# Attention 2: where the next group's weights are split, and on which engine their low parts are made

## The chip, the cores and the metric

The kernel runs on one core of a Trainium2 chip. Its metric is the device time of one execution, in microseconds. The kernel before takes 973.61 us, the median of three runs (972.61 to 974.28).

A core has five instruction streams that run at the same time and meet only at semaphores: TensorE (PE in the profile, its weight loads are PEld), VectorE (DVE), ScalarE (ACT), GpSimd (POOL) and SyncE (SP), which here only issues DMAs. Each stream runs its instructions in the order in which they were written. An instruction that waits holds up all that stands behind it on its engine.

## The reference, cut to what matters

The program is a small transformer layer in float32: attention 1, then a feed-forward part that is itself a second attention (attention 2) with a mixture of experts behind it. The change touches only attention 2:

```
h = rmsnorm(hidden, ln1_w)                       # 4 batches x 256 rows x 256
q = rope((h @ Wq).reshape(B, S, 32, 128));  k = rope((h @ Wk).reshape(B, S, 4, 128));  v = h @ Wv
k, v = repeat(k, 8), repeat(v, 8)                # 8 query heads share a key head
attn = softmax(mask(q @ k.T / sqrt(128)))        # causal, 256 x 256 per head
x = hidden + (attn @ v) @ Wo
```

There are 32 query heads of width 128, in 4 groups of 8 that share a key and value head. Wq is 256 x 4096, Wo is 4096 x 256.

## The kernel before

**Products of three.** Float32 accuracy on TensorE is had by splitting each operand into a high part (rounded to fp32r) and a low part (what is left): `three()` (lines 70 to 75) makes each product from low*high, high*low and high*high. So each operand that TensorE reads passes two engines first: ScalarE copies it to the rounded type, then another engine subtracts the copy from the original. The attention weights are such an operand too.

**Iterations and slots.** Attention 2 runs 16 iterations: 4 groups of heads, and in each the 4 batches. An iteration has 4 pairs of heads, so there are 64 slots P = 0 to 63. In this text "slot 12" is P = 12, and "a slot of kind 3" is one with P mod 4 = 3. A group is 16 slots: 0 to 15, 16 to 31, 32 to 47, 48 to 63. The methods `slot_pe`, `slot_act`, `slot_dve` and `slot_pool` write out by hand what each engine does in slot P, for pairs at different stages:

- TensorE: scores of pair P; in kinds 0 and 1 the keys and values of the next iteration (`pe_kv` KV0, KV1); the output projection of pair P-5; probabilities times values of P-4; in kind 3 the transpose of the next iteration's keys (KT, line 1177); the queries of P+3 (`pe_queries`); the transpose of the probabilities of P-2 (line 518).
- ScalarE: the copy of the transposed probabilities; the high part of the rotated queries of P+1 (line 1155); the exponentials of P (line 1297); key and value copies; the high part of the outputs (line 1336); in kind 3 the high part of the transposed keys (line 1199); the raw copy of the queries of P+3 (line 1118).
- VectorE: the row maxima of P (line 1284), the low parts of the transposed probabilities (line 643) and of the queries of P+1 (line 1160), the reciprocals of P-1 (line 619), the low parts of the outputs (line 1341) and in kind 3 of the transposed keys (line 1210), the cosine product of the queries of P+3 (line 1138), in kind 3 the low part of the values (line 1248), in kind 0 an addition to the accumulator (line 1352).
- GpSimd: the normalisation of P-1 (line 637), which waits for the reciprocals; the two halves of the rotation of the queries of P+2 (line 1146, which waits for a swap by DMA, and line 1150); in kinds 1 and 2 the rotation of the next keys (lines 1224, 1229).
- SyncE: for each pair a swap of the two halves of its 128 partitions by two DMAs (`sp_swap`, line 1126), all in one queue.

**The weights of the next group.** `b_w` holds the split weights of two groups (the one in use and the next), `b_w_raw` the raw weights of one. A group's weights are 4608 columns, split in quarters of 1152 columns. SyncE loads the raw weights (`load_weights`: four DMAs, line 1478); `act_weights` (line 1367) makes the high part of a quarter, at the end of each slot of kind 2; `pool_weights` (line 1371) makes its low part on GpSimd, at the end of each slot of kind 3: slots 3, 7, 11 and 15 of a group. The load for group g+1 stands in SyncE's order ahead of the swap of pair 19 or 35, behind the last quarter of the group before. In slot 12 of a group TensorE reaches KV0 of the next group's first iteration (line 1181) and in slot 13 its queries (line 1103); both wait until three of the four quarters are ready. The projection with the new weights, which wants the fourth, comes in slot 21.

Of the kernel before, what the change touches and what calls it, by code (L numbers as in the profile page):

```python
# [37 lines left out]
NB, SEQ, D = 4, 256, 256  # L38
# [6 lines left out]
HPI, PAIRS = 8, 4  # L45
# [6 lines left out]
KV, DH = 4, 128  # L52
B_ITS = NB * KV
# [10 lines left out]
def wait(eng, sem, value):  # L64

    if isinstance(value, int) and value <= 0:
        return
    eng.wait_ge(sem, value)
# [635 lines left out]
class AttentionA(Attention):  # L704
# [186 lines left out]
    def act_weights(self, act, it):  # L891
        pass
# [137 lines left out]
class AttentionB(Attention):  # L1030
# [8 lines left out]
    KT_AT = 3  # L1039
    ROPE_AT = {1: KV0, 2: KV1}  # L1040
    SWAPPED = 32

    def __init__(self, m, ctx):
        super().__init__(m, ctx, "b_")
# [97 lines left out]
    def pool_rotate(self, pool, P):  # L1142
        nc = self.m.nc
        wait(pool, self.swapped[P % 2], self.SWAPPED * (P // 2 + 1))
        sin = self.pairs_of(self.swp, P)
# [210 lines left out]
    def quarter(self, it, part=None):  # L1356
# [4 lines left out]
        at = ((it // NB + 1) % 2) * (2 * B_W) + q + part * B_W  # L1361
        return self.w[:, at:at + WQUART]

    def act_weights(self, act, it):
        wait(act, self.w_loaded, 16 * W_DMAS * (it // NB + 1))
        wait(act, self.w_done, PAIRS * (it - 2) + 1)
        self.m.nc.scalar.activation(self.quarter(it, 0), self.quarter(it), ACT.Copy).then_inc(self.w_hi, 1)

    def pool_weights(self, pool, it):
        wait(pool, self.w_hi, it + 1)  # L1370
        self.m.nc.gpsimd.tensor_tensor(self.quarter(it, 1), self.quarter(it),
                                       self.quarter(it, 0).bitcast(F32),
                                       ALU.subtract).then_inc(self.w_ready, 1)

    def more_weights(self, it):
        return it < B_ITS - NB

    def at(self, P):
        return P // PAIRS, P % PAIRS, P
# [24 lines left out]
    def slot_act(self, act, P):  # L1404
        it, p = P // PAIRS, P % PAIRS
        if self.runs(P - 3):
            self.act_prob_t(act, (P - 3) % PAIRS, P - 3)
        if self.runs(P + 1):
            self.act_queries(act, P + 1)
        if self.runs(P):  # L1410
            self.act_exp(act, p, P)
        if it + 1 < self.ITS and p in self.KV_AT:
            self.act_kv(act, it + 1, self.KV_AT[p])
        if self.runs(P - 4):
            self.act_outputs(act, *self.at(P - 4))
        if it + 1 < self.ITS and p == self.KT_AT:
            self.act_kv(act, it + 1, self.KT)
        if self.runs(P + 3):
            self.act_raw(act, P + 3)
        if self.runs(P) and p == PAIRS - 1:  # L1420
            self.act_values(act, it)
        if p == PAIRS - 2 and self.more_weights(it):
            self.act_weights(act, it)

    def slot_dve(self, dve, P):
        it, p = P // PAIRS, P % PAIRS
        if self.runs(P):
            self.dve_max(dve, p, P)
        if self.runs(P - 3):
            self.dve_prob_t(dve, (P - 3) % PAIRS, P - 3)  # L1430
        if self.runs(P + 1):
            self.dve_queries(dve, P + 1)
        if self.runs(P - 1):
            self.dve_normalise(dve, (P - 1) % PAIRS, P - 1)
        if it + 1 < self.ITS and p in self.KV_AT:
            self.dve_kv(dve, it + 1, self.KV_AT[p])
        if self.runs(P - 4):
            self.dve_outputs(dve, *self.at(P - 4))
        if it + 1 < self.ITS and p == self.KT_AT:
            self.dve_kv(dve, it + 1, self.KT)  # L1440
        if self.runs(P + 3):
            self.dve_cos(dve, P + 3)
        if self.runs(P) and p == PAIRS - 1:
            self.dve_values(dve, it)
        if p == 0 and it >= 2:
            self.dve_add(dve, it - 2)

    def slot_pool(self, pool, P):
        it, p = P // PAIRS, P % PAIRS
        if self.runs(P - 1):  # L1450
            self.pool_normalise(pool, (P - 1) % PAIRS, P - 1)
        if self.runs(P + 2):
            self.pool_rotate(pool, P + 2)
        if it + 1 < self.ITS and p in self.ROPE_AT:
            self.pool_kv(pool, it + 1, self.ROPE_AT[p])
        if p == PAIRS - 1 and self.more_weights(it):
            self.pool_weights(pool, it)

    TAIL = 7

# [8 lines left out]
    def build(self, dram):  # L1469
# [3 lines left out]
        @block.sync  # L1473
        def _(sp):
            def load_weights(g):
                wait(sp, self.w_ready, 4 * g)
                for dst, src in group_weights(m, dram, g):
                    sp.dma_start(dst, src).then_inc(self.w_loaded, 16)

            load_weights(1)  # L1480
            for P in range(self.STAGES):
                slot = P - 3
                if slot > 0 and slot % (PAIRS * NB) == 0 and slot // (PAIRS * NB) < KV - 1:
                    load_weights(slot // (PAIRS * NB) + 1)
                self.sp_swap(sp, P)
            sp.wait_ge(self.w_ready, 4 * KV)
            for dst, src in expert_weights(m.e_w_raw, dram, 0):
                sp.dma_start(dst, src).then_inc(self.e_loaded, 16)
# [664 lines left out]
```

## Time and profile before

| what | value |
|---|---|
| median of the runs | 973.61 us |
| the profiled execution | 973.91 us |
| its span (first to last instruction) | 972.0 us |
| PE busy | 880.8 us (91%) |
| DVE busy | 614.8 us (63%) |
| ACT busy | 571.7 us (59%) |
| POOL busy | 482.4 us (50%) |
| attention 2, slots 0 to 63 | about 214 to 635 us of the span |

The profile comes from one execution. "Busy" counts a matmul from its start to its modelled end. The trace also gives the clock that was granted to TensorE, in each stretch as a share of the full 2.4 GHz: 1.00 is full speed, 0.50 is 1.2 GHz. A slot begins with the first score matmul of its pair (line 73, `banks<-b_kt,b_qt`), so its length is the distance to the next such row. In the stretch that the change touches, TensorE is the engine without idle time in most slots; the others have some in each.

### The profile page before, as it was taken

How to read it: one execution, taken by the hardware profiler on the slowest of the kernel's cores; microseconds unless marked ns; L12 is line 12 of the kernel's file. 1: busy time of each engine (PE TensorE's matmuls, PEld its weight loads, DVE VectorE, ACT ScalarE, POOL GpSimd, SP SyncE). 2: the span in 40 equal slices, each digit the busy share in tenths (PEclk: the TensorE clock that was granted, in tenths of full speed). 3: DMA queues.
4: the chain of work that ended last, by engine and by line, in shares of the span. 5: the costliest groups of instructions: out<-in, count | busy, mean ns of one | idle time of the engine just before them, and what ended most of it. 6: DMA issues, size and time to landing. Idle time of an engine off the chain costs nothing. (4 is left out here: it accounts for less than half of the span.)

```text
span 972.0 us, 18784 instructions
## 1 busy us (share of the span) xinstructions
PE 880.8 (91%) x6108; PEld 817.0 (84%) x6108; DVE 614.8 (63%) x1608; ACT 571.7 (59%) x1572; POOL 482.4 (50%) x492
## 2 busy tenths in 40 slices
PE   3699999467998999899998999978999999999994
PEld 2599898457998999898998999967888888888884
DVE  7356666755776777676786777763544545445456
ACT  4788888455775577576775676754333333333333
POOL 5633334256886788777886877730122222222221
PEclk9899999778999999899999999995999999999998
DMA  6000100311111411114111111200343333333231
GB/s 207 23 1 24 43 22 1 98 33 45 44 41 32 137 39 39 33 45 130 44 45 34 45 35 44 61 1 17 104 129 109 106 109 113 113 113 109 98 95 44
DMA packets 50246, 63.34 MB, mean 65 GB/s; under 512 B 5728, under 2 KB 36064, under 8 KB 50176
## 3 DMA queue, kind: packets, MB, share of 16 engines
q1 hardware_dynamic: 49088, 61.41, 21.8%
q10 hardware_dynamic: 1088, 1.05, 0.3%
q8 instruction: 37, 0.61, 0.3%
q14 instruction: 33, 0.27, 0.1%
HBM read 41.86 MB, written 1.18 MB: 44 GB/s over the span
## 5 line engine op out<-in xcount | busy, mean ns | idle before, releaser
L637 POOL TENSOR_TENSOR b_prob<-b_prob,b_rsum 128x256 f32<-128x256 f32 (+1 forms) x128 | 103.9, 832 | 88.6 <-DVE b_rsum L619 88.6
L73 PE MATMUL banks<-act_t,b_w 128*128 128x256 f32 (+1 forms) x392 | 129.9, 331 | 2.0 <-DVE moe_hid L1985 1.1
L75 PE MATMUL banks<-act_t,b_w 128*128 128x256 f32 (+1 forms) x392 | 127.7, 326 | 0.0
L74 PE MATMUL banks<-act_t,b_w 128*128 128x256 f32 (+1 forms) x392 | 127.6, 326 | 0.0
L1889 ACT ACTIVATE moe_hid<-banks 128x512 fp32r<-128x512 f32 x66 | 39.4, 597 | 123.9 <-DVE banks L1980 123.9
L1297 ACT ACTIVATE b_prob<-banks,b_negmax 128x128 f32<-128x128 f32 (+1 forms) x256 | 103.2, 414 | 7.6 <-DVE b_negmax L1284 7.6
L1973 DVE TENSOR_TENSOR moe_gated<-banks,moe_share 128x512 f32<-128x512 f32 x66 | 45.6, 691 | 85.4 <-PE banks L75 81.7
L637 POOL TENSOR_TENSOR a_prob<-a_prob,a_rsum 128x256 f32<-128x256 f32 x64 | 51.6, 827 | 82.7 <-DVE a_rsum L619 82.7
L1146 POOL TENSOR_TENSOR b_work<-b_work,rope_t 128x512 f32<-128x512 f32 x64 | 83.5, 1305 | 13.9 <-DMA b_work<-b_work 13.9
L1155 ACT ACTIVATE b_qt<-b_work 128x512 fp32r<-128x512 f32 x64 | 40.4, 632 | 82.9 <-POOL b_work L1150 82.9
L1150 POOL TENSOR_TENSOR b_work<-b_work 128x512 f32<-128x512 f32 x64 | 83.7, 1308 | 9.2
L1284 DVE CUSTOM_DVE_ANT_0 banks<-banks,mask_neg 128x128 f32<-128x128 f32 (+1 forms) x256 | 83.8, 389 | 5.6 <-PE banks L75 2.1
L73 PE MATMUL banks<-b_kt,b_qt 128*128 128x128 f32 (+1 forms) x256 | 77.2, 301 | 7.0 <-issue 3.0
L73 PEld LDWEIGHTS banks<-act_t,b_w 128*128 128x128 f32 x392 | 75.9, 194 | 7.2 <-DVE moe_hid L1985 1.3
L73 PE MATMUL banks<-b_w,b_ot 128*128 128x256 f32 x256 | 75.9, 296 | 6.2 <-DVE b_ot L1341 6.1
L75 PEld LDWEIGHTS banks<-act_t,b_w 128*128 128x128 f32 x392 | 75.6, 193 | 6.1
L74 PEld LDWEIGHTS banks<-act_t,b_w 128*128 128x128 f32 x392 | 75.9, 194 | 4.8
L1341 DVE TENSOR_TENSOR b_ot<-banks,b_ot 128x512 fp32r<-128x512 f32 x64 | 44.0, 688 | 56.6 <-ACT b_ot L1336 56.5
L75 PE MATMUL banks<-b_w,b_ot 128*128 128x256 f32 x256 | 74.9, 293 | 0.0
L74 PE MATMUL banks<-b_w,b_ot 128*128 128x256 f32 x256 | 74.9, 293 | 0.0
L1985 DVE TENSOR_TENSOR moe_hid<-banks,moe_hid 128x512 fp32r<-128x512 f32 x66 | 45.7, 692 | 45.4 <-ACT moe_hid L1889 45.4
L1936 POOL TENSOR_TENSOR b_w<-b_w_raw,b_w 128x512 fp32r<-128x512 f32 x16 | 20.7, 1297 | 108.0 <-ACT b_w L1875 108.0
(229 smaller groups left out, 3085.6 us busy)
## 6 DMA issues: line engine op xcount, KB each, us to landing
b_work<-b_work SPq DMA_DIRECT2D x128, 128.0 KB, 2.3
moe_share<-gates SPq DMA_DIRECT2D x32, 512.0 KB, 3.7
b_w_raw<-in_b_wq SPq DMA_DIRECT2D x4, 1024.0 KB, 5.3
b_w_raw<-in_b_wo SPq DMA_DIRECT2D x4, 1024.0 KB, 9.0
a_src_t<-act_t SPq DMA_DIRECT2D x5, 512.0 KB, 2.9
moe_w_raw<-in_wg SPq DMA_DIRECT2D x16, 128.0 KB, 2.2
moe_w_raw<-in_wu SPq DMA_DIRECT2D x16, 128.0 KB, 2.2
moe_w_raw<-in_wd SPq DMA_DIRECT2D x16, 128.0 KB, 2.3
```

The source lines that it names most:

```text
L73: nc.tensor.matmul(out, w_lo, m_hi, start=start, stop=False, skip_group_check=skip)
L74: nc.tensor.matmul(out, w_hi, m_lo, start=False, stop=False, skip_group_check=skip)
L75: return nc.tensor.matmul(out, w_hi, m_hi, start=False, stop=stop, skip_group_check=skip)
L637: last = self.m.nc.gpsimd.tensor_tensor(rows, rows, rsum[:, :, t:t + 1].to_broadcast([PART, 2, width]), ALU.mult)
L1146: nc.gpsimd.tensor_tensor(sin, sin, self.q_table(1), ALU.mult).then_inc(self.sin_ready, 1)
L1150: nc.gpsimd.tensor_tensor(total, total, self.swp[:, P % 2, :], ALU.add).then_inc(self.q_added, 1)
L1155: self.m.nc.scalar.activation(self.qt[:, P % PAIRS, 0, :], self.cos_part[:, P % 2, :], ACT.Copy).then_inc(self.qt_hi, 1)
L1284: last = nc.vector.tensor_tensor_reduce(row, row, m.mask_neg[:, SEQ - width:SEQ], 1.0, -NEG, ALU.add, ALU.min, accum_out=self.negmax[:, p ...
L1297: last = nc.scalar.activation(self.prob[:, p, h, lo:lo + width], m.s_ps[:, h, lo:lo + width], ACT.Exp, bias=self.negmax[:, p % 2, t, h:h + ...
L1341: self.m.nc.vector.tensor_tensor(self.ot[:, p % 2, 1, :], self.m.o_ps[:], self.ot[:, p % 2, 0, :].bitcast(F32), ALU.subtract).then_inc(sel ...
L1973: nc.vector.tensor_tensor(gated[n][:], gu[n][1], share[par][:, n * half:(n + 1) * half], ALU.mult).then_inc(gated_done, 1)
L1985: nc.vector.tensor_tensor(hid[n][:, 1, :], gu[n][0], hid[n][:, 0, :].bitcast(F32), ALU.subtract).then_inc(hid_ready, 1)
```

## The change

The low parts move from GpSimd to VectorE (`dve_weights`), and the places move: ScalarE makes the high parts at the end of slots 1, 4, 7 and 10 of a group, and VectorE the low parts one slot later, at the end of slots 2, 5, 8 and 11. The load of the group after next moves up in SyncE's order, from ahead of the swap of pair 19 (35) to ahead of the swap of pair 16 (32). ScalarE's waits are written for the new places.

```diff
--- before.py
+++ after.py
@@ -1039,6 +1039,7 @@
     KT_AT = 3
     ROPE_AT = {1: KV0, 2: KV1}
     SWAPPED = 32
+    SPLIT_AT = {1: 0, 4: 1, 7: 2, 10: 3}
 
     def __init__(self, m, ctx):
         super().__init__(m, ctx, "b_")
@@ -1361,19 +1362,27 @@
         at = ((it // NB + 1) % 2) * (2 * B_W) + q + part * B_W
         return self.w[:, at:at + WQUART]
 
+
+
+
     def act_weights(self, act, it):
         wait(act, self.w_loaded, 16 * W_DMAS * (it // NB + 1))
-        wait(act, self.w_done, PAIRS * (it - 2) + 1)
+        wait(act, self.q_full, PAIRS * NB * (it // NB))
+        if it % NB >= 2:
+            wait(act, self.w_done, PAIRS * NB * (it // NB))
         self.m.nc.scalar.activation(self.quarter(it, 0), self.quarter(it), ACT.Copy).then_inc(self.w_hi, 1)
 
-    def pool_weights(self, pool, it):
-        wait(pool, self.w_hi, it + 1)
-        self.m.nc.gpsimd.tensor_tensor(self.quarter(it, 1), self.quarter(it),
+    def dve_weights(self, dve, it):
+        wait(dve, self.w_hi, it + 1)
+        self.m.nc.vector.tensor_tensor(self.quarter(it, 1), self.quarter(it),
                                        self.quarter(it, 0).bitcast(F32),
                                        ALU.subtract).then_inc(self.w_ready, 1)
 
-    def more_weights(self, it):
-        return it < B_ITS - NB
+    def quarter_at(self, P):
+
+        g, slot = P // (PAIRS * NB), P % (PAIRS * NB)
+        split = self.SPLIT_AT.get(slot)
+        return None if split is None or not 0 <= g < KV - 1 else NB * g + split
 
     def at(self, P):
         return P // PAIRS, P % PAIRS, P
@@ -1419,8 +1428,8 @@
             self.act_raw(act, P + 3)
         if self.runs(P) and p == PAIRS - 1:
             self.act_values(act, it)
-        if p == PAIRS - 2 and self.more_weights(it):
-            self.act_weights(act, it)
+        if (q := self.quarter_at(P)) is not None:
+            self.act_weights(act, q)
 
     def slot_dve(self, dve, P):
         it, p = P // PAIRS, P % PAIRS
@@ -1444,6 +1453,8 @@
             self.dve_values(dve, it)
         if p == 0 and it >= 2:
             self.dve_add(dve, it - 2)
+        if (q := self.quarter_at(P - 1)) is not None:
+            self.dve_weights(dve, q)
 
     def slot_pool(self, pool, P):
         it, p = P // PAIRS, P % PAIRS
@@ -1453,8 +1464,6 @@
             self.pool_rotate(pool, P + 2)
         if it + 1 < self.ITS and p in self.ROPE_AT:
             self.pool_kv(pool, it + 1, self.ROPE_AT[p])
-        if p == PAIRS - 1 and self.more_weights(it):
-            self.pool_weights(pool, it)
 
     TAIL = 7
 
@@ -1480,8 +1489,8 @@
             load_weights(1)
             for P in range(self.STAGES):
                 slot = P - 3
-                if slot > 0 and slot % (PAIRS * NB) == 0 and slot // (PAIRS * NB) < KV - 1:
-                    load_weights(slot // (PAIRS * NB) + 1)
+                if slot > 0 and slot % (PAIRS * NB) == 13 and slot // (PAIRS * NB) < KV - 2:
+                    load_weights(slot // (PAIRS * NB) + 2)
                 self.sp_swap(sp, P)
             sp.wait_ge(self.w_ready, 4 * KV)
             for dst, src in expert_weights(m.e_w_raw, dram, 0):
```

On VectorE, at the seam of slots 2 and 3 of the first group, the order before is this (ISA is the row maximum with its read-out):

```order
L1160 TENSOR_TENSOR b_qt<-b_work,b_qt 128x512 [waits b_qt_hi]
L619 RECIPROCAL b_rsum<-b_sums 128x4 [waits b_exp_done]
L1138 TENSOR_TENSOR b_work<-banks,rope_t 128x512 [waits b_qt_ready,b_raw_ready]
L1284 ISA banks,b_negmax<-banks,mask_neg 128x128 [waits b_s_full,b_exp_done]
L1284 ISA b_negmax 128x1
```

and after the change it is this:

```order
L1161 TENSOR_TENSOR b_qt<-b_work,b_qt 128x512 [waits b_qt_hi]
L619 RECIPROCAL b_rsum<-b_sums 128x4 [waits b_exp_done]
L1139 TENSOR_TENSOR b_work<-banks,rope_t 128x512 [waits b_qt_ready,b_raw_ready]
L1377 TENSOR_TENSOR b_w<-b_w_raw,b_w 128x1152 [waits b_w_hi]
L1285 ISA banks,b_negmax<-banks,mask_neg 128x128 [waits b_s_full,b_exp_done]
L1285 ISA b_negmax 128x1
```

The subtraction of a quarter now stands between the cosine product of a slot and the maxima of the next. The seams of slots 5/6, 8/9 and 11/12 look the same, with the accumulator's addition (8/9) or the low part of the values (11/12) between the cosine product and the quarter.

On GpSimd, at the seam of slots 3 and 4, the order before is this:

```order
L1146 TENSOR_TENSOR b_work<-b_work,rope_t 128x512 [waits b_swapped1]
L1150 TENSOR_TENSOR b_work<-b_work 128x512 [waits b_sin_ready,b_cos_ready]
L1371 TENSOR_TENSOR b_w<-b_w_raw,b_w 128x1152 [waits b_w_hi]
L637 TENSOR_TENSOR b_prob<-b_prob,b_rsum 128x2x128 [waits b_rsum_ready]
L637 TENSOR_TENSOR b_prob<-b_prob,b_rsum 128x2x256
```

and after the change this:

```order
L1147 TENSOR_TENSOR b_work<-b_work,rope_t 128x512 [waits b_swapped1]
L1151 TENSOR_TENSOR b_work<-b_work 128x512 [waits b_sin_ready,b_cos_ready]
L637 TENSOR_TENSOR b_prob<-b_prob,b_rsum 128x2x128 [waits b_rsum_ready]
L637 TENSOR_TENSOR b_prob<-b_prob,b_rsum 128x2x256
```

The quarter is gone from the end of the slot, and nothing takes its place. On TensorE the order is unchanged.

## Rows read from the trace of the kernel before

**Rows 1.** TensorE's waits, 205 to 590 us: total us, times, longest us.
```profile
PE banks L73 <- POOL b_w L1371: 9.5, 3, 3.2
```
**Rows 2.** Stretches: length, busy PE, PEld, DVE, ACT, POOL, TensorE clock, DMA share, GB/s.
```profile
568.47:575.12 6.65, 6.65 (x54) 6.53 (x55) 5.47 (x15) 4.40 (x15) 4.59 (x5) 1.00 0.17 39
581.78:587.73 5.95, 5.95 (x52) 5.83 (x50) 4.25 (x13) 4.14 (x13) 4.83 (x7) 1.00 0.19 44
587.73:594.03 6.30, 6.30 (x54) 6.08 (x52) 4.67 (x14) 4.54 (x15) 5.31 (x7) 1.00 0.19 44
289.72:301.33 11.61, 8.41 (x56) 8.08 (x55) 6.67 (x15) 4.65 (x15) 8.79 (x7) 0.85 0.10 23
400.63:413.23 12.60, 9.41 (x55) 8.91 (x55) 6.33 (x15) 4.64 (x15) 8.82 (x7) 0.73 0.10 22
512.32:523.77 11.45, 8.34 (x55) 8.00 (x55) 6.16 (x15) 4.55 (x15) 8.75 (x7) 0.85 0.11 24
333.56:349.08 15.52, 14.26 (x101) 13.41 (x100) 9.56 (x28) 9.47 (x27) 10.67 (x13) 0.89 0.22 53
445.67:460.91 15.24, 13.12 (x101) 12.02 (x100) 9.54 (x29) 9.88 (x29) 10.69 (x13) 1.00 0.21 50
```
**Rows 3.** The same view, of a stretch in slot 12 behind its wait.
```profile
295.00:298.40 3.40, 3.40 (x18) 3.40 (x17) 0.75 (x3) 0.45 (x2) 3.06 (x4) 0.50 0.00 0
```
**Rows 4.** Instructions by tile or line: duration ns min/median/max, first and last start.
```profile
L1371 POOL TENSOR_TENSOR b_w<-b_w_raw,b_w x12: 2607/2689/2891, 239.8 to 544.9; 128x1152 fp32r<-128x1152 f32 x12
...
L1160 DVE TENSOR_TENSOR b_qt<-b_work,b_qt x64: 678/782/2331, 212.4 to 634.9; 128x512 fp32r<-128x512 f32 x64
```
**Rows 5.** Timeline (start us, duration us), VectorE and GpSimd meeting, three times.
```profile
291.87 2.61 POOL L1371 TENSOR_TENSOR b_w<-b_w_raw,b_w 128x1152 fp32r<-128x1152 f32 x1
292.89 2.13 DVE L1160 TENSOR_TENSOR b_qt<-b_work,b_qt 128x512 fp32r<-128x512 f32 x1
...
433.21 1.33 DVE L1248 TENSOR_TENSOR b_v<-b_v_row,b_v 128x256 fp32r<-128x256 f32 x1
434.21 2.89 POOL L1371 TENSOR_TENSOR b_w<-b_w_raw,b_w 128x1152 fp32r<-128x1152 f32 x1
...
594.76 0.41 DVE L1248 TENSOR_TENSOR b_v<-b_v_row,b_v 128x256 fp32r<-128x256 f32 x1
594.85 1.47 POOL L1150 TENSOR_TENSOR b_work<-b_work 128x512 f32<-128x512 f32 x1
```
**Rows 6.** Timeline: from GpSimd's rotation to the next scores, slots 23 and 55.
```profile
369.75 1.30 POOL L1150 TENSOR_TENSOR b_work<-b_work 128x512 f32<-128x512 f32 x1
...
374.97 0.30 PE L73 MATMUL banks<-b_kt,b_qt 128*128 128x128 f32 x1 [0.22 <-issue]
...
588.82 1.29 POOL L1150 TENSOR_TENSOR b_work<-b_work 128x512 f32<-128x512 f32 x1
...
593.51 0.41 DVE L1210 TENSOR_TENSOR b_kt<-banks,b_kt 128x256 fp32r<-128x256 f32 x1
...
594.03 0.30 PE L73 MATMUL banks<-b_kt,b_qt 128*128 128x128 f32 x1
```
**Rows 7.** Timeline: the seams 53/54, 54/55 and 56/57, two engines.
```profile
582.04 0.69 DVE L1138 TENSOR_TENSOR b_work<-banks,rope_t 128x512 f32<-128x512 f32 x1 [0.73 <-ACT b_work L1118]
...
582.66 1.29 POOL L1150 TENSOR_TENSOR b_work<-b_work 128x512 f32<-128x512 f32 x1
...
587.38 1.30 POOL L1146 TENSOR_TENSOR b_work<-b_work,rope_t 128x512 f32<-128x512 f32 x1
...
601.12 1.30 POOL L1150 TENSOR_TENSOR b_work<-b_work 128x512 f32<-128x512 f32 x1
...
601.54 0.68 DVE L1352 TENSOR_TENSOR acc<-banks,acc 128x512 f32<-128x512 f32 x1
```
**Rows 8.** Timeline: SyncE's load for the third group, and GpSimd in slot 18.
```profile
325.20 0.37 SPq L1478 DMA_DIRECT2D b_w_raw<-in_b_wq  x1
...
336.42 1.30 POOL L1146 TENSOR_TENSOR b_work<-b_work,rope_t 128x512 f32<-128x512 f32 x1 [3.06 <-DMA b_work<-b_work]
```

## The prediction, on record before the changed kernel ran

> **What bounds the kernel now.** I read TensorE's waits first. Between 205 and 590 us one line leads: three waits for the subtraction of a weight quarter on GpSimd, 9.5 us in all, 3.2 at most [rows 1]. TensorE is busy 91% of the span, so I then asked for busy times slot by slot, to see how much of a wait reaches the slot's length. Slots that nothing disturbs show TensorE busy from end to end: slot 52 takes 6.65 us, slots 54 and 55 take 5.95 and 6.30 (the first three of [rows 2]). TensorE is the bound there, and every idle moment of it is lost. Slots 12, 28 and 44, the ones in which the weights of the next group are first used, take 11.61, 12.60 and 11.45 (the next three of [rows 2]). Slots 18 and 19 together take 15.52, slots 34 and 35 15.24, against 12.25 for 54 and 55 (the last two of [rows 2]). These are the two places that the change can win at.
>
> The excess in slot 12 is more than its wait. Behind the wait TensorE's granted clock is 0.50 for 3.40 us, its 1.2 GHz level, while its queue is full [rows 3]; work for 1.7 us is done there in 3.4. Slot 12 has 0.85 as its mean clock, slot 28 0.73, slot 44 0.85 [rows 2]. So an idle TensorE of 3 us costs 1.7 us or more on top.
>
> Last I read the timelines of GpSimd and VectorE side by side, for what a subtraction costs on VectorE and what it does to its neighbours.
>
> **What goes.** (a) The quarter that slots 12, 28 and 44 wait for is made at the end of slot 11 on GpSimd; it will be made at the end of slot 8 on VectorE. The waits go whole: (11.61 - 6.65) + (12.60 - 6.65) + (11.45 - 6.65) = 4.96 + 5.95 + 4.80 = 15.7 us, the slow clock included. What is late next there is nothing of slot 12 itself: slot 52 does the same work from the same kind of order in 6.65.
>
> (b) The loads. The first of the weight DMAs of the third group is issued at 325.20; the swap of pair 19 is queued behind all four, and GpSimd waits 3.06 us until it has landed at 336.42 [rows 8], 11.2 us after that issue. Slots 18/19 and 34/35 lose 15.52 - 12.25 = 3.3 and 15.24 - 12.25 = 3.0 by it. The new place is behind the swap of pair 15, about 1 us into slot 13, and the next swap, that of pair 16, is asked for one slot later. If its landing is again 11.2 us after the load's first issue, that is 12.2 - 6.65 = 5.6 us into slot 14. GpSimd wants it in slot 14 where line 1146 stands in slot 54: 587.38 - 581.78 = 5.60 [rows 2, 7]. That just meets. I count the whole 6.3 us as won; the bounds are 0 and 6.3 of it back, since a later landing on another queue order isn't in the trace. The buffer is free in time, since the fourth quarter ends in slot 11.
>
> Twelve subtractions of 2.69 us also leave GpSimd [rows 4]. It is no bound in an undisturbed slot (4.83 of 5.95), so this alone wins nothing. The twelve activations of ScalarE stay as they are; at their new places ScalarE next waits for GpSimd's line 1150 as before. I cost them at nothing; without that cover each would cost its length, below the 2.69 of its GpSimd partner.
>
> **What comes.** Twelve subtractions of 1152 columns on VectorE, with both inputs in SBUF. The trace has that kind with 512 columns at 0.68 us (the least of line 1160) [rows 4] and with 256 columns at 0.41 [rows 5]; a column costs 0.27/256 = 1.05 ns, so 1152 columns take 0.68 + 640 x 1.05 ns = 1.35 us (estimate from these rows; 1.2 to 1.6).
>
> They do not run beside GpSimd. While GpSimd made a quarter (291.87 to 294.48), line 1160 took 2.13 us in place of 0.68 and ended 0.54 behind it. The other way, line 1150 took 1.47 in place of 1.29 when it started 0.09 behind a subtraction of 256 columns. And at 433.21 a waiting VectorE got in between two GpSimd instructions: it took 1.33, and the quarter behind it 2.89 in place of 2.61 [rows 5]. So one waits for the other's whole instruction, and who has waited goes first. A quarter that has waited ends some 1.2 us after its release.
>
> The Trainium skill says this as a rule ("SBUF — State Buffer", the section on the two separate sides): VectorE with two SBUF inputs and GpSimd reading SBUF exclude each other for a whole instruction, the first to start wins. The trace agrees (2.13 against 0.68). If they only shared a bandwidth, the seams below would cost about half, some 7 us in all, and the time would be about 959.
>
> Why this reaches TensorE: in a slot of kind 3 everything hangs on GpSimd's line 1150 in that slot's first half. Behind it come, in order, ScalarE's high part of the queries, the exponentials, the outputs' and the keys' high parts, and VectorE's low part of the keys (593.51 + 0.41), and the scores of the next slot start 0.11 later. From the end of line 1150 to those scores it is 594.03 - 590.11 = 3.92 us in slot 55, and 374.97 - 371.05 = 3.92 in slot 23 [rows 6]. So in kind 3, a microsecond by which line 1150 is late is a microsecond of the kernel. A quarter makes it late directly, or through VectorE's maxima, behind which stand the reciprocals that GpSimd's next normalisation waits for.
>
> Seam 2/3, as 54/55. The quarter is asked for 0.87 into slot 3 (cosine product 0.26 into the slot and 0.61 long, as in slot 54 [rows 2, 7]), that is 588.60 here. Line 1146 holds GpSimd until 588.68; then the quarter is first, until 589.9, and line 1150, due at 588.82, is 0.95 late. Cost 0.95 in slot 3.
>
> Seam 5/6, as 53/54. The quarter is asked for at 582.65, line 1150 starts at 582.66: nobody can say who wins. VectorE first: line 1150 and the maxima are each late by 1.1, and so are reciprocals, normalisation and line 1150 of slot 6, which slot 7 pays: 1.1. GpSimd first: the quarter ends at 583.95 + 1.2, the maxima are 2.2 late: 2.2. I take the middle, 1.6.
>
> Seam 8/9, as 56/57. The addition (601.54) lets the quarter ask at 602.14, inside line 1150 (601.12 to 602.42) [rows 7]. It ends at 603.6 and the maxima are 1.4 late. GpSimd has slack in slot 9, but its normalisation waits for the reciprocals, so line 1150 of slots 9 and 10 is 1.3 late; slot 11 pays 1.3 (1.2 to 1.4).
>
> Seam 11/12, as 55/56. Line 1150 waits behind the values' subtraction (594.76) already and goes first, until 596.32 [rows 5]; the quarter ends at 597.5, the maxima are 2.3 late. Slots 12 and 13 have slack for about half; 1.1 is left in slot 14's line 1150, and slot 15 pays. If VectorE keeps its turn instead it is 0.1. I take 1.1, as the row at 433.21 has the one that waited go first.
>
> Sum per group: 0.95 + 1.6 + 1.3 + 1.1 = 4.95 (3.3 to 5.7); three groups have it: 14.9 us (10 to 17). Below nothing it can't be, since nothing in these seams gets earlier.
>
> The clock. TensorE's new waits come about 1 us at a time, most split in two (for the transposed keys' rows, then for the scores). One like it is in slots 18 and 19, whose mean clock is 0.89; slots 34 and 35 had such waits at 1.00 [rows 2]. I count one fall of 1.7 us in the twelve places; the bounds are none and all twelve, 0 to 20 us.
>
> **The sum.** The profiled execution took 973.91 us (span 972.0 and 1.9 around it), 0.3 above the median of the runs. 973.9 - 15.7 - 6.3 + 14.9 + 1.7 = 968.5; less 0.3 is 968.2. I say 968.
>
> **The rivals.**
> 1. Hidden seams: VectorE is busy 4.25 to 5.47 us of each slot, so 1.35 more fits. Then only the gains count: 973.6 - 22.0 = 951.6. Against it stands the fixed 3.92 behind line 1150. 0.1.
> 2. Cheap seams: VectorE wins seam 5/6, seam 11/12 is free, no fall of the clock: 973.6 - 22.0 + 10 = 961.6. 0.25.
> 3. The load's stall only moves to slots 14 and 15, (a) alone does what it says: 968.2 + 6.3 = 974.5. For it: the meeting of 5.6 and 5.60; against it: normalisations that come late in slot 14 give it another microsecond. 0.1.
> 4. Slower: at each of the twelve seams the wait is followed by half clock, as in rows 3. Without a fall the sum is 973.6 - 22.0 + 14.9 = 966.5; a fall costs 1.7, so four bring it back to 973.3, from six on (976.7) it is over 0.2% slower, and with all twelve and dear seams (17) it is 973.6 - 22.0 + 17 + 20 = 988.6. Against it: the waits in slots 34 and 35 had none. 0.1.
>
> The forecast has 0.45. From no change, a measurement of this kernel can tell about 0.2%, 2 us. Faster by more: forecast, 1 and 2, 0.8. Within: most of 3, 0.1. Slower: 4, 0.1. The range leaves out rival 1 and most of rival 4: 958 to 976.
>
> **What would show it.** Right: TensorE's waits have no line for the quarter, and slots 12, 28 and 44 take about 6.7. The load's DMAs stand about 18 us ahead of their old place in the program, and slots 18 and 34 take 5.95. Quarters of VectorE take 1.35 alone and up to 2.6 where a GpSimd instruction lies under their start. Slots 3, 7, 11 and 15 of a group take 7.2, 7.4 to 8.5, 7.6 and 7.4 in place of 6.3 to 6.6, still 3.92 behind line 1150. Wrong: if kind 3 stays at 6.3 to 6.6 (rival 1), if GpSimd waits for a swap in slot 14 (rival 3), if many stretches of slots 3 to 47 stand at 0.50 (rival 4), or if slots of kinds 0 to 2 grow, which I have at nothing.

## The result, and the profile after

| | before | after |
|---|---|---|
| median of the runs | 973.5 us (972.61 to 974.28, 4 runs) | 961.33 us (961.08 to 963.52, 4 runs) |
| ratio | | 0.988 [0.9863, 0.9897] |
| the profiled execution, its span | 973.91, 972.0 | 961.15, 959.1 |
| DVE busy, POOL busy | 614.8, 482.4 | 624.5, 456.0 |

The change saves 12.2 us; 5.6 were forecast. The time lies in the range and near rival 2 (961.6), but not for rival 2's reasons, as the slots show.

TensorE's waits between 205 and 590 us (total us, times, longest us) answer to [rows 1]. Lines in the changed file stand one to nine lower, so line 1150 is 1151 here, and a quarter's low part is line 1377:

```profile
PE banks L1178 <- POOL b_k_row L1230: 11.3, 12, 4.7
PE banks L73 <- issue: 6.2, 12, 2.5
...
PE banks L73 <- DVE b_qt L1161: 1.1, 1, 1.1
```

No line names a quarter any more. In its place stand waits in kind 3: in each of these slots one for the rows of the keys that are to be transposed (the first line, twelve times) and, from slot 7 on, one of about 0.34 us in front of the next scores (eleven of the twelve in the second line; the 2.5 is ahead of slot 0). Before, the first of these lines had 4.5 us in 2 waits; 3.7 of that, and 4.7 here, is one wait in slot 3, the first of its kind.

The busy times of single slots (columns as in [rows 2]): slots 12, 18 and 19, then the kind-3 slots 7, 27, 15, 23 and 43:

```profile
290.61:297.26 6.65, 6.65 (x54) 6.53 (x55) 6.40 (x16) 3.89 (x14) 2.44 (x3) 1.00 0.18 41
330.46:336.41 5.95, 5.95 (x51) 5.82 (x50) 4.25 (x13) 5.09 (x14) 4.82 (x7) 1.00 0.20 47
336.41:343.70 7.29, 6.63 (x54) 6.09 (x52) 5.88 (x16) 4.93 (x16) 6.30 (x7) 1.00 0.15 36
256.24:263.80 7.56, 6.62 (x54) 6.09 (x52) 5.44 (x16) 5.44 (x17) 6.57 (x8) 1.00 0.15 35
390.63:398.18 7.55, 6.62 (x54) 6.09 (x52) 5.45 (x16) 6.49 (x18) 6.56 (x8) 1.00 0.15 35
309.87:317.16 7.29, 6.63 (x54) 6.09 (x52) 5.44 (x16) 5.07 (x16) 6.25 (x8) 1.00 0.16 36
363.13:371.37 8.24, 6.61 (x53) 6.07 (x52) 5.43 (x16) 5.19 (x17) 7.23 (x9) 1.00 0.15 35
498.13:505.94 7.81, 6.65 (x53) 6.12 (x52) 5.45 (x16) 6.74 (x20) 6.82 (x9) 1.00 0.15 34
```

Slot 12 is down from 11.61 to 6.65 [rows 2], and 28 and 44 take 6.65 too. From slot 7 on, each kind-3 slot idles TensorE for 0.6 to 1.6 us, and the granted clock stays at 1.00 in all eleven. (Slot 3 idles it for 4.7 at a mean clock of 0.67; before it was 3.7, and 0.71.)

Two seams on the timeline of VectorE and GpSimd (start, duration). Seam 18/19, the one called 2/3 above:

```profile
336.06 1.30 POOL L1147 TENSOR_TENSOR b_work<-b_work,rope_t 128x512 f32<-128x512 f32 x1
337.50 2.27 POOL L1151 TENSOR_TENSOR b_work<-b_work 128x512 f32<-128x512 f32 x1
...
337.27 1.35 DVE L1377 TENSOR_TENSOR b_w<-b_w_raw,b_w 128x1152 fp32r<-128x1152 f32 x1
...
343.70 0.30 PE L73 MATMUL banks<-b_kt,b_qt 128*128 128x128 f32 x1 [0.34 <-issue]
```

The quarter takes 1.35 alone, as estimated. Line 1151 takes 2.27, for 1.30 in peace: it waits 0.97 for the quarter and ends at 339.77, and the next scores come 3.93 behind it, against 3.92 in [rows 6]. Slot 19 is 0.99 over 6.30; 0.95 was forecast. Slot 3 pays nearly the same (0.9), but by another way: there the quarter itself waits and takes 2.37. Seam 5/6 shows the tie, first slot 6, then slot 22:

```profile
251.51 2.32 POOL L1151 TENSOR_TENSOR b_work<-b_work 128x512 f32<-128x512 f32 x1
...
251.34 1.34 DVE L1377 TENSOR_TENSOR b_w<-b_w_raw,b_w 128x1152 fp32r<-128x1152 f32 x1
...
357.79 1.28 POOL L1151 TENSOR_TENSOR b_work<-b_work 128x512 f32<-128x512 f32 x1
359.04 1.57 POOL L1225 TENSOR_TENSOR b_k_sin<-b_k_raw,rope_sb 128x128 f32<-128x128 f32 x1
...
357.87 2.43 DVE L1377 TENSOR_TENSOR b_w<-b_w_raw,b_w 128x1152 fp32r<-128x1152 f32 x1
```

In slot 6 VectorE was 0.17 ahead: its quarter took 1.34, line 1151 2.32, and slot 7 was 1.26 over 6.30. In slot 22 GpSimd was 0.08 ahead: the quarter took 2.43, and then GpSimd's next instruction waited in its turn (1.57 for 0.46). Slots 22 and 23 were 2.12 over.

Where the 12.9 us between the two profiled spans went shows by stretches: before (start of slot 0 to slot 3, slots 3 to 47, slots 48 to 61, the rest),

```profile
213.74:229.56 15.82, 13.76 (x91) 13.36 (x91) 9.52 (x34) 7.41 (x31) 7.59 (x8) 0.81 0.18 42
229.56:542.67 313.11, 295.93 (x2286) 286.36 (x2287) 229.18 (x640) 211.91 (x624) 240.90 (x240) 0.96 0.22 54
542.67:630.31 87.64, 87.48 (x703) 85.15 (x703) 68.21 (x198) 61.03 (x187) 65.26 (x68) 1.00 0.20 48
630.31:971.98 341.67, 318.81 (x1827) 280.54 (x1825) 176.20 (x338) 134.43 (x265) 79.11 (x79) 0.96 0.28 90
```

and after:

```profile
213.37:227.94 14.57, 12.49 (x91) 12.09 (x91) 10.41 (x34) 8.48 (x32) 7.62 (x8) 0.88 0.20 46
227.94:532.39 304.45, 289.44 (x2287) 278.89 (x2287) 239.45 (x653) 208.75 (x624) 217.25 (x229) 0.99 0.22 56
532.39:619.78 87.39, 87.37 (x702) 85.15 (x703) 66.78 (x198) 60.72 (x185) 62.26 (x67) 1.00 0.20 48
619.78:959.07 339.29, 316.41 (x1827) 278.26 (x1825) 176.62 (x338) 134.65 (x265) 79.16 (x79) 0.97 0.28 90
```

The changed part, slots 3 to 47, gives 8.7 us. The other 4.2 in these two profiles come from 0.4 ahead of slot 0, 1.3 in slots 0 to 2, 0.2 in slots 48 to 61 and 2.4 behind them. In the last stretch both kernels run the same 1827 matmuls, with VectorE and ScalarE equally busy; only TensorE's clock differs, 0.96 against 0.97.

### The profile page after: what moved, and what is told of

It reads as the page before. It is cut to its first block and busy times, and to the rows that moved or that the text cites. A ratio compares the mean times of both kernels' runs of the same rounds, so it can differ in the third digit from the quotient of the medians.

```text
span 959.1 us, 18782 instructions
## 1 busy us (share of the span) xinstructions
PE 870.1 (91%) x6108; PEld 804.9 (84%) x6108; DVE 624.5 (65%) x1620; ACT 569.9 (59%) x1572; POOL 456.0 (48%) x480
## 5 line engine op out<-in xcount | busy, mean ns | idle before, releaser
L1151 POOL TENSOR_TENSOR b_work<-b_work 128x512 f32<-128x512 f32 x64 | 86.6, 1353 | 9.5 <-DVE b_work L1139 0.4
L73 PE MATMUL banks<-b_w,b_ot 128*128 128x256 f32 x256 | 73.1, 286 | 5.6 <-DVE b_ot L1342 5.6
L75 PE MATMUL banks<-b_w,b_ot 128*128 128x256 f32 x256 | 72.4, 283 | 0.0
L74 PE MATMUL banks<-b_w,b_ot 128*128 128x256 f32 x256 | 72.3, 283 | 0.0
```

Source lines behind the costliest of these rows:

```text
L73: nc.tensor.matmul(out, w_lo, m_hi, start=start, stop=False, skip_group_check=skip)
L74: nc.tensor.matmul(out, w_hi, m_lo, start=False, stop=False, skip_group_check=skip)
L75: return nc.tensor.matmul(out, w_hi, m_hi, start=False, stop=stop, skip_group_check=skip)
L1151: nc.gpsimd.tensor_tensor(total, total, self.swp[:, P % 2, :], ALU.add).then_inc(self.q_added, 1)
```

## The experiments

My theory: each quarter on VectorE excludes GpSimd and so makes line 1151 late, which kind 3 pays; the earlier load ended the stalls of slots 18 and 34. Rivals: the seams' cost is VectorE's occupied time, whatever it reads; the load's place does nothing. In this section "slots 3 to 47" is that stretch's length: 313.1 before, 304.5 after.

**The load back at its old place**, in the changed kernel.

```diff
-                if slot > 0 and slot % (PAIRS * NB) == 13 and slot // (PAIRS * NB) < KV - 2:
-                    load_weights(slot // (PAIRS * NB) + 2)
+                if slot > 0 and slot % (PAIRS * NB) == 0 and slot // (PAIRS * NB) < KV - 1:
+                    load_weights(slot // (PAIRS * NB) + 1)
```

> The changed kernel with the load's DMAs back at their old place, ahead of the swaps of pairs 19 and 35. Theory: the load's place is worth the 6.3 us that slots 18/19 and 34/35 lost before, so 967.6 us (966 to 968.5), and the excess is in slots 18 and 19 (34 and 35) again, GpSimd waiting about 3 us for a swap in slot 17 (33). Rival: the gain of the change beyond the forecast comes from the load, so that it is worth 9 us or more here: 970 or above. Second rival: the lateness of the new seam 18/19 covers the swap's, and only 3 us come back: 964.

Measured: 962.73 us (961.35 to 962.88), ratio 0.9887 [0.9868, 0.9906]. Slots 3 to 47 take 304.45 as in the changed kernel, slot 18 takes 5.95 and slot 19 7.28. The forecast of 967.6 was a miss by 5 us. So the place of the load wins nothing here; moving the fourth quarter was enough. SyncE's queue says why (issue time and duration of its DMA instructions):

```profile
311.28 7.46 SPq L1127 DMA_DIRECT2D b_work<-b_work  x4
318.79 0.59 SPq L1487 DMA_DIRECT2D b_w_raw<-in_b_wq  x1
...
324.87 20.41 SPq L1127 DMA_DIRECT2D b_work<-b_work  x8
```

At the same place in the order, the load is issued at 318.79 and the swap behind it at 324.87, 6 us later. In the kernel before the load went at 325.20 [rows 8] and the swap of pair 19 at 327.98, right behind it:

```profile
322.49 2.69 POOL L1371 TENSOR_TENSOR b_w<-b_w_raw,b_w 128x1152 fp32r<-128x1152 f32 x1
327.98 22.36 SPq L1126 DMA_DIRECT2D b_work<-b_work  x8
```

SyncE had stood at the load's own wait for the fourth quarter, which GpSimd finished only at 325.18.

**The quarters at the new places, but on GpSimd.**

```diff
-        if (q := self.quarter_at(P - 1)) is not None:
-            self.dve_weights(dve, q)
...
+        if (q := self.quarter_at(P - 1)) is not None:
+            self.pool_weights(pool, q)
```

> The changed kernel, its places and its load as they are, but the low parts made by GpSimd (2.7 us each, at the end of GpSimd's slots 2, 5, 8 and 11). Theory: the place alone takes away the waits of slots 12, 28 and 44; GpSimd's quarter pushes its own line 1150 of the next slots: seam 2/3 costs 0 (line 1150 of slot 2 is already done), 5/6 costs 1.8, 8/9 0.8, 11/12 0.3, so 2.9 a group against 5.1 measured with VectorE: 961.3 - 6.6 = 954.7 us (951 to 958). Rival: leaving GpSimd is what gains, GpSimd becomes the bound of every kind 3: 965 or above.

Measured: 964.73 us (962.61 to 965.82), ratio 0.9915 [0.9896, 0.9934]; slots 3 to 47 take 305.6. A miss by 10 us. The gain of (a) came, but the seams were as dear on GpSimd. Put beside the three profiles of the changed kernel (304.5, 305.5 and 304.8 in slots 3 to 47), this says that nearly all of the gain is the places'; what the other engine adds is 0.1 to 1.2 us of that stretch, about as much as these three differ among themselves, and the medians (964.7 against 961.3 and, later, 961.9) leave it 3 us or so. The dearest seam is 5/6; slot 23, and GpSimd in front of it:

```profile
364.49:373.71 9.22, 7.34 (x53) 7.02 (x52) 5.18 (x16) 4.93 (x16) 8.23 (x10) 0.89 0.13 29
```

```profile
362.07 3.11 POOL L1377 TENSOR_TENSOR b_w<-b_w_raw,b_w 128x1152 fp32r<-128x1152 f32 x1
365.14 1.61 POOL L637 TENSOR_TENSOR b_prob<-b_prob,b_rsum 128x256 f32<-128x256 f32 x2
...
368.15 1.27 POOL L1151 TENSOR_TENSOR b_work<-b_work 128x512 f32<-128x512 f32 x1
```

The quarter starts 3.5 us into slot 22 and takes 3.11; the normalisation starts 0.65 into slot 23 and line 1151 3.66 into it, where line 1150 stood 1.41 into slot 23 of the kernel before (369.75 [rows 6]): 2.3 later. The mean clock is 0.89. GpSimd has room on average (4.83 of 5.95 us busy [rows 2]) but no hole of 2.7 us at the seam 5/6; at 8/9 and 11/12 its quarter costs less than VectorE's (1.7 and 2.1 us in all, against 4.0 and 2.8).

**One SBUF input in place of two.** VectorE reads the quarter with a reduction of the same 1152 columns. It also writes one column where the subtraction wrote 1152. This kernel does not make the low parts of the next groups' weights.

```diff
-        self.m.nc.vector.tensor_tensor(self.quarter(it, 1), self.quarter(it),
-                                       self.quarter(it, 0).bitcast(F32),
-                                       ALU.subtract).then_inc(self.w_ready, 1)
+        self.m.nc.vector.tensor_reduce(self.sink[:], self.quarter(it), AX, ALU.max).then_inc(self.w_ready, 1)
```

> The changed kernel with each subtraction on VectorE replaced by a maximum over the same 1152 columns, an instruction of about the same length with one SBUF input; the low parts of the weights of groups 2 to 4 are not made. Theory: a good half of the seams' cost is that VectorE and GpSimd exclude each other when VectorE reads two SBUF inputs. Then line 1150 always takes 1.29, the reductions 1.2 to 1.3 us, seam 2/3 costs 0, 5/6 1.1 in every group (8.24 us slots gone), 8/9 1.2, 11/12 0.1: 2.4 a group, 961.3 - 8 = 953.3 us (951 to 956). Rival: VectorE's own time makes the lateness, whatever it reads: 960 to 962.

Measured: 956.17 us (954.58 to 958.69), ratio 0.9829 [0.9804, 0.9854]; slots 3 to 47 take 297.7, 6.8 less than after. The time is 0.2 above the expected range. VectorE at seam 18/19, then the slots 19, 23, 27 and 31:

```profile
336.71 1.34 DVE L1378 TENSOR_REDUCE b_sink<-b_w_raw 128x1 f32<-128x1152 f32 x1
```

```profile
335.85:342.15 6.30, 6.30 (x53) 6.07 (x51) 5.75 (x15) 4.55 (x15) 4.38 (x6) 1.00 0.18 42
361.41:368.75 7.34, 6.62 (x54) 6.09 (x52) 4.94 (x15) 4.92 (x16) 6.35 (x8) 1.00 0.16 37
388.00:395.45 7.45, 6.63 (x53) 6.10 (x52) 5.44 (x16) 6.36 (x18) 6.46 (x8) 1.00 0.15 35
414.71:421.31 6.60, 6.41 (x54) 6.08 (x52) 4.95 (x15) 4.84 (x16) 5.61 (x7) 1.00 0.17 40
```

The reduction occupies VectorE just as long, 1.34. Seam 2/3 is gone and 11/12 nearly (0.3 in slot 31, nothing in slot 47; slot 15 takes 7.44, but there GpSimd waits 1.09 for a swap behind the load); 5/6 keeps 1.04 to 1.20 and 8/9 about 1.15. Of the seams' 15.2 us 8.2 are left. So both mechanisms are real and are told apart: where GpSimd's rotation meets the quarter itself, the exclusion is the cost; where the delay goes through the maxima and the reciprocals, VectorE's time alone costs 1.1.

That the second input makes the exclusion, and not the 1152 columns written, this run alone doesn't show. VectorE's cosine product does: it writes 512 columns to SBUF, with one input in SBUF and one in PSUM. In the changed kernel 26 of its 64 executions lie wholly inside an instruction of GpSimd, and none is longer than 0.694 us:

```profile
L1139 DVE TENSOR_TENSOR b_work<-banks,rope_t x64: 673/691/694, 201.2 to 615.3; 128x512 f32<-128x512 f32 x64
```

**Other slots for the quarters.** High parts in kind 3, low parts in kind 0, ahead of VectorE's work on the probabilities.

```diff
-    SPLIT_AT = {1: 0, 4: 1, 7: 2, 10: 3}
+    SPLIT_AT = {0: 0, 4: 1, 8: 2, 12: 3}
...
+        if P and (q := self.quarter_at(P)) is not None:
+            self.dve_weights(dve, q)
         if self.runs(P - 3):
             self.dve_prob_t(dve, (P - 3) % PAIRS, P - 3)
```

> The changed kernel with the low parts in slots 0, 4, 8 and 12 of a group, behind the maxima (high parts at the end of the slot before; in the first group the first quarter behind the keys' cosine product), the load unchanged. GpSimd stands idle there for 1.9 us, and the slots of kind 0 have over 2.4 us of slack on VectorE. Theory: line 1150 of the slots of kind 2 is on time again, slots of kind 3 take 6.3 to 6.5, all of the seams' 15 us come back: 946.5 us (945 to 949). Rival: a quarter on VectorE costs TensorE about its length wherever it stands: 960 to 962.

Measured: 953.34 us (952.01 to 955.09), ratio 0.979 [0.977, 0.9809]; slots 3 to 47 take 293.7, 10.7 less than after. The forecast was 946.5, all of the seams' 15; a miss by 7 us. Here are slots 15, 19, 23 and 47:

```profile
310.16:317.95 7.79, 6.62 (x53) 6.09 (x52) 4.94 (x15) 4.92 (x16) 5.67 (x7) 1.00 0.15 36
337.20:343.50 6.30, 6.30 (x53) 6.08 (x52) 4.67 (x14) 4.55 (x15) 5.31 (x7) 1.00 0.18 42
362.76:369.06 6.30, 6.30 (x53) 6.08 (x52) 4.66 (x14) 4.54 (x15) 5.31 (x7) 1.00 0.18 43
517.16:523.46 6.30, 6.30 (x53) 6.08 (x52) 4.66 (x14) 4.54 (x15) 5.31 (x7) 1.00 0.19 43
```

Behind the new places kind 3 is at 6.30, with three exceptions. Slot 7 takes 7.31, here and in the next two kernels; its quarter stands in slot 4, right behind TensorE's 3.7 us wait in slot 3, and in the other groups the same order costs nothing. No run takes this apart. Slot 15 is late since GpSimd waits for a swap that is queued behind the load,

```profile
311.29 1.30 POOL L1147 TENSOR_TENSOR b_work<-b_work,rope_t 128x512 f32<-128x512 f32 x1 [1.43 <-DMA b_work<-b_work]
```

and slot 31 has 0.97 of the same, while slot 47, where no load is, has none. That is rival 3's mechanism. In the first profile of the changed kernel it does not show: GpSimd comes 0.6 us later to this place, since the seam has delayed it already, and finds the swap landed (310.50). It shows in the second and third,

```profile
313.17 1.30 POOL L1147 TENSOR_TENSOR b_work<-b_work,rope_t 128x512 f32<-128x512 f32 x1 [0.70 <-DMA b_work<-b_work]
```

```profile
311.13 1.30 POOL L1147 TENSOR_TENSOR b_work<-b_work,rope_t 128x512 f32<-128x512 f32 x1 [0.39 <-DMA b_work<-b_work]
```

and slot 15 takes 7.97 and 7.66 there, against 7.29 in the first. Their loads were first issued at 300.84 and 299.12, so the swap lands 12.3 and 12.0 us behind that; the forecast had 11.2 from slot 18.

**The load ahead of the swap of pair 17**, on top of the last.

```diff
-                if slot > 0 and slot % (PAIRS * NB) == 13 and slot // (PAIRS * NB) < KV - 2:
+                if slot > 0 and slot % (PAIRS * NB) == 14 and slot // (PAIRS * NB) < KV - 2:
```

> The kernel with the low parts in the slots of kind 0, with the load's DMAs ahead of the swap of pair 17 (33) in place of 16 (32). In its trace slots 15 and 31, the ones behind a load, still take 7.79 and 7.27 where slot 47, without a load, takes 6.30. Theory: the load holds up the swap that GpSimd wants in slot 14, whose line 1150 has no slack, while the swap of pair 17 is wanted in slot 15, whose line 1150 has 1.9 us; so slots 15 and 31 take 6.3, and the time is 953.3 - 2.5 = 950.8 us (949.5 to 952). Rival: the load slows these slots wherever it is put: 953.

Measured: 951.53 us (948.87 to 954.27), ratio 0.9777 [0.975, 0.9804]; slots 3 to 47 take 293.2. Slots 15 and 31 are at 6.30, but slot 17 grew to 7.91, since the late swap and the quarter of slot 16 now meet line 1151. Little is won: the expected 950.8 lies inside the runs' spread (948.87 to 954.27), but of the 2.5 us that slots 15 and 31 gave, slots 17, 19 and 35 took back 2.0.

**The same, with VectorE's quarter behind the reciprocals and the normalisation's release**, late in kind 0.

```diff
         if self.runs(P - 1):
             self.dve_normalise(dve, (P - 1) % PAIRS, P - 1)
+        if P and (q := self.quarter_at(P)) is not None:
+            self.dve_weights(dve, q)
```

> As the kernel before this one (low parts in kind 0, load ahead of the swap of pair 17), but each quarter behind the reciprocals in place of behind the maxima. There GpSimd's normalisation is just released, and the quarter is ahead of it. Theory (they exclude each other, and the slots of kind 0 have slack for 1.3 us either way): within 0.7 us of it, 951 us, with GpSimd's first normalisation longer by about 1.1 us in these slots. Rival: the collision costs TensorE about 1 us in each slot of kind 3 behind, 11 in all: 960 or more.

Measured: 950.41 us (946.53 to 951.77), ratio 0.978 [0.9758, 0.9803]; slots 3 to 47 take 291.0, 13.4 less than the changed kernel. The expected 951 was met. This is the best version of the study in that stretch; by the ratios it can't be told from the one before (0.978 and 0.9777). All twelve quarters, and slots 15, 19 and 23:

```profile
L1377 DVE TENSOR_TENSOR b_w<-b_w_raw,b_w x12: 1318/1329/1354, 218.6 to 497.8; 128x1152 fp32r<-128x1152 f32 x12
```

```profile
308.12:314.41 6.29, 6.29 (x54) 6.08 (x52) 4.66 (x14) 4.54 (x15) 4.72 (x6) 1.00 0.86 266
333.67:340.31 6.64, 6.41 (x53) 6.07 (x52) 5.12 (x16) 4.89 (x16) 5.65 (x8) 1.00 0.17 39
359.58:365.88 6.30, 6.30 (x53) 6.07 (x52) 4.67 (x14) 4.55 (x15) 5.31 (x7) 1.00 0.19 43
```

No quarter waits for GpSimd, as in the two kernels before this one. The two engines still exclude each other: GpSimd's first normalisation takes 1.64 us behind eleven of the quarters, for 0.6 in peace, as expected. It has that time to spare there. In the changed kernel line 1377 reads:

```profile
L1377 DVE TENSOR_TENSOR b_w<-b_w_raw,b_w x12: 1342/2034/2439, 229.7 to 506.8; 128x1152 fp32r<-128x1152 f32 x12
```

**The swap ahead of the load**, in the kernel before and nothing else, to test the cause of the stall in slots 18 and 34.

```diff
-                if slot > 0 and slot % (PAIRS * NB) == 0 and slot // (PAIRS * NB) < KV - 1:
+                if slot > 1 and slot % (PAIRS * NB) == 1 and slot // (PAIRS * NB) < KV - 1:
```

> The kernel before, with one edit: the load of the next group's weights stands ahead of the swap of pair 20 (36), not of pair 19 (35). The weights are split as before, on GpSimd in slots 3, 7, 11 and 15 of a group. Two theories on what slots 18/19 and 34/35 lost in the kernel before. Order theory: the loss came because SyncE waited for the fourth quarter until 325.20 and then sent the load and, right behind it, the swap of pair 19 (327.98), whose data waited behind the load's in the queue; with the swap ahead of the load slot 18 takes 5.95 (before 7.19), slot 19 about 6.4 (8.33), slots 34/35 the same, slots 12, 28 and 44 stay at 11.4 to 12.6, and the time is 973.5 - 6 = 967.5. SyncE theory: the swap was late by itself because SyncE stood at the wait until 325.20; this stays (the swap of pair 19 is issued behind the same wait or a little after), so the loss halves at most and the time is 970.5 or more. A third outcome, that ScalarE at the end of slot 18 waits for the later load, would show as a wait of ScalarE on DMA in slot 18 and a slot 19 above 7.

Measured: 964.93 us (964.44 to 965.72, 6 runs), ratio 0.992 [0.9904, 0.9937]. Slots 3 to 47 take 307.6, 5.6 less than before. GpSimd's waits for swaps between 320 and 350 us, before and here:

```profile
POOL b_work L1146 <- DMA b_work<-b_work: 3.1, 1, 3.1
```

```profile
POOL b_work L1146 <- DMA b_work<-b_work: 0.5, 1, 0.5
```

Slots 18 and 34 take 5.95 and slots 12, 28 and 44 still 11.67, 11.53 and 12.57. The order theory holds: the stall was the swap's place right behind the load. Of the 6.3 us that slots 18/19 and 34/35 had lost, 5.1 come back. Slot 19 takes 7.11, above what that theory gave: line 1150 starts 0.8 later in it than in slot 55, 0.5 of it by the wait above, for the next swap, which now stands behind the load. No DMA holds ScalarE there.

**Both kernels once more**, for the part outside the slots.

> The kernel before, unchanged, for a second trace. Of the 12.8 us between the two traces, slots 3 to 47 hold 8.7; 1.3 stand in slots 0 to 2 and 2.4 behind slot 61, where the two programs are the same, with other places of the half clock. Theory: where the clock falls at the joins of the stages is chance: slots 0 to 2 take 14.5 or 15.8 and the stretch behind slot 61 339 to 342 us, in either kernel, so this trace shows one of them different from the first (341.7). Rival: the change moves it: again 15.8 and 341.7.

> The changed kernel once more, for a second trace. Theory: slots 3 to 47 take 304.5 within 0.5; slots 0 to 2 and the stretch behind slot 61 take what the clock's falls leave, 14.5 to 15.8 and 339 to 342 us. Rival: 14.6 and 339.3 again.

> The changed kernel once more, to see how far the part of the gain that lies outside slots 3 to 47 (4.2 us between the two profiles of before and after) is the change's. If it is: ratio 0.988 again and the stretch from start to slot 3 and from slot 48 to the end 730 to 731 in total. If it is a chance of the clock at the joins of stages, the time moves between 961 and 965 from run to run, the ratio comes out between 0.987 and 0.992, and slots 3 to 47 stay at 304.4 to 305.5 whatever the rest does.

(These stretches add up to 654.6 in the first profile of after; the 730 to 731 of the last expectation is a slip.)

Measured: before 970.99 us in its one run; after 964.44 in one, then 961.88 (959.82 to 965.42, 5 runs), ratio 0.9899 [0.9876, 0.9922]. The second profile of before, slots 0 to 2 and the last stretch, to compare with the first and fourth row of before above:

```profile
213.69:228.30 14.61, 12.56 (x90) 12.15 (x91) 9.38 (x34) 7.41 (x30) 7.60 (x8) 0.88 0.18 41
629.70:969.10 339.40, 316.38 (x1827) 278.43 (x1824) 176.25 (x338) 134.47 (x265) 79.11 (x79) 0.97 0.28 90
```

The same kernel now has the numbers of after. And after's second profile has 15.83 in slots 0 to 2, which is before's number. Slots 3 to 47 hardly move: 313.1 and 313.7 before; 304.5, 305.5 and 304.8 after. What is outside them is 658.9 and 655.4 before, 654.6, 657.0 and 653.0 after, and 653.5 to 659.4 in the experiments, in no order of theirs. So most of the 4.2 us is chance of the execution. Not all of it need be: the 30 runs of before have a mean of 972.8 (median 972.7), the ten of after 962.3 (961.7). That is 10.4 to 11 us, about 2 more than the 8.5 by which slots 3 to 47 differ on average. No version's quarters or load go with these 2 us: the mean of the runs, less 2 us around the span and less slots 3 to 47, gives an estimate of 657.4 outside them for before and 655.4 for after, but 655.4 for the kernel that only swaps the order of load and swap, and up to 657.7 for those with the quarters on VectorE. What makes them is open.

## Why the prediction was wrong

| step | forecast us | measured us |
|---|---|---|
| (a) slots 12, 28, 44 | -15.7 | -15.7 |
| (b) slots 18/19, 34/35 | -6.3 | -6.3 |
| seams 2/3, in slots 3, 19, 35 | +2.85 | +2.86 |
| seams 5/6, in slots 7, 22/23, 38/39 | +4.8 | +5.5 |
| seams 8/9, in slots 11, 27, 43 | +3.9 | +4.0 |
| seams 11/12, in slots 15, 31, 47 | +3.3 | +2.8 |
| kind 3 above 6.30 before | 0 | -1.3 |
| slot 4 | 0 | -0.6 |
| falls of the clock | +1.7 | 0 |
| slots 3 to 47 | -5.4 | -8.7 |
| outside them | 0 | -4.2 |

The measured seams are the excess of those slots over 6.30 (5.95 in slots 22 and 38); for slot 3 it is 10.48 - 9.59.

- **(a) was right**, to 0.1 us, the half clock behind the waits included.
- **(b) was right in size and wrong in cause.** The prediction gave it to the load's new place. It was the fourth quarter that came early enough for SyncE: with the load put back the slots don't change, and in the kernel before the order of swap and load alone gives 5.1 of it. I read that GpSimd waited for the swap [rows 8], but did not ask what SyncE itself had waited for until 325.20. The new place even has a price: 0.4 and 0.7 us in slot 15 in two of the three profiles of after, and 1.5 and 1.0 in slots 15 and 31 once the seams are gone.
- **The seams were right**, 15.2 against 14.9, and so was the way they reach TensorE. The tie was the one place with no number of its own: 1.6 was between 1.1 and 2.2, and the three groups gave 1.26, 2.12 and 2.12. One reading in them was off without harm: the rows give the cosine product 0.69 us, not 0.61; the next instruction of VectorE starts 0.60 behind its start (336.67 and 337.27 in the changed kernel), and that is what the sum needed. The Trainium skill's rule ("SBUF — State Buffer", two separate sides), that VectorE with two SBUF inputs and GpSimd exclude each other, holds in this case's traces: with one SBUF input and the same length 7.0 of the 15.2 go. The forecast of about 959 (960, if the fall of the clock is left in as in the sum) by shared bandwidth lies near the measured median, but only as a total; the seams themselves cost whole instructions.
- **The failed step is the sum, in three terms that it set without a row of their own.** With (a), (b) and the seams right, the saving was forecast too small by these three:
  - *What lies outside slots 3 to 47, set at nothing.* It was 4.2 us shorter in the two profiles, the largest of the three. Some of that is chance: the profiled execution of before was 3.5 us slower there than its second profile. Over all runs about 2 us stay, and their cause is open.
  - *The clock, set at one fall, 1.7 us.* None came in slots 5 to 61 in any of the three profiles of after. TensorE's idle time was at most 1.6 us a slot there.
  - *Kind 3 before the change, taken as 6.30.* It already took up to 0.33 more in eight slots of before ([rows 2] shows only undisturbed ones). I charged the seams from 6.30 and so paid that part, 1.3 us in all, twice.
- Slot 4's 0.6 is chance, since the second profile of before has 5.22 there as after has.

Rival 1 fell (the seams are not hidden), rival 4 fell (no half clock). Rival 2 named the time, with cheap seams; they were not cheap, so its 961.6 beside 961.33 is luck. Rival 3's wait exists, but the seams cover most of it.

## What to carry to other kernels

Ask first what moved. The title names two changes, place and engine; with the quarters back on GpSimd at the new places nearly all of the gain stayed. A low part on VectorE costs TensorE nothing only where neither GpSimd's next instruction nor VectorE's own next one is urgent; look for the place behind which a chain has slack (here late in kind 0, behind the reciprocals), not for the engine with the lowest busy share. Four quarters a group cost 5 us at the seams and, late in kind 0, 1 or less. Where a transfer is late, ask what its queue's engine had waited for, and what stands right behind a big load in the same queue: swapping two DMA issues gave 7.4 us of 972 by the medians, 5.6 of them in slots 3 to 47. And before a term is charged from an undisturbed slot, compare that slot with the very ones it is charged to.

## What the runs showed of the hardware

- Idle time of TensorE of 0.6 to 1.6 us a slot, in two waits of at most 1.3, eleven times in each of three profiles, was followed by no fall of the granted clock. But such waits don't exclude one: behind a wait of 1.0 us slot 19 of before had a mean of 0.80, and behind one of 1.3 slot 35 of its second profile 0.79. In slot 23 of the version with GpSimd quarters TensorE was idle for 1.9 us and the mean was 0.89, in slot 39 for 2.3 us at 1.00. Behind waits of about 3 us it was 0.73 to 0.85 in all three slots [rows 2].
- A start 0.08 or 0.17 us earlier decides which of VectorE and GpSimd waits, and with it 0.9 us of the kernel. And who has waited makes the other wait next (line 1225: 1.57 in place of 0.46 behind a quarter that had waited).
- Equal instruction counts with equal work take 337.3 to 342.2 us in the last stretch from execution to execution, as the mean granted clock of that stretch goes from 0.97 to 0.96. A single profile's span is good to some 4 us here, its changed stretch to 1.
